# Probabilities transposed into the score banks, and each group's work in another order

## The reference

```
xn = ln(x, g_norm)
q = l2norm(heads(xn @ Wq)) * q_scale;  k, v = split(xn @ Wkv);  k = l2norm(k) * k_scale
sim = 8 * q @ k.T + bias;   causal mask;   attn = softmax(sim)       # 16 heads, 256 x 257
y = ln((attn @ v) @ Wout, g_out)
out = x + down(quant(silu(gate(quant(y))) * up(quant(y))))
```

## Time and profile before

| | |
|---|---|
| median of 3 runs | 312.78 us (311.99 to 313.17) |
| the profiled execution | 312.39 us; its span (first to last instruction) 310.6 us |
| busy share of the span | TensorE 83%, VectorE 78%, ScalarE 73%, GpSimd 67% |
| granted TensorE clock, mean | 0.98 |
| values of groups 2 to 33 | from 38.6 to 270.6 us |

### The profile page before, as it was taken

How to read it: one execution, slowest core, us unless ns; L and a number is a source line. 1 busy time by engine, 2 the same in 40 slices (tenths; PEclk the granted TensorE clock), 3 DMA queues, 4 the chain that set the end, 5 groups by cost and what they waited for, 6 DMA issues and landing times.

```text
span 310.6 us, 7321 instructions
## 1 busy us (share of the span) xinstructions
PE 258.5 (83%) x2175; PEld 203.0 (65%) x2176; DVE 242.8 (78%) x967; ACT 226.9 (73%) x779; POOL 207.2 (67%) x394
## 2 busy tenths in 40 slices
PE   0668899999989998999899989999999987776260
PEld 0337677777877786778777877788778766561050
DVE  2989688777888788878877987787877766759993
ACT  1265689778877887788888878888788868448480
POOL 2789867777777777777777777777777655212301
PEclk9999999999999999999999999999999999999956
DMA  4279000000000000000000000000000020000013
GB/s 142 51 179 251 1 0 3 2 0 3 1 2 0 4 1 2 0 3 1 2 2 1 4 0 2 0 4 0 2 1 3 1 72 1 2 0 0 1 36 106
DMA packets 13083, 6.89 MB, mean 22 GB/s; under 512 B 1953, under 2 KB 12913, under 8 KB 13042
## 3 DMA queue, kind: packets, MB, share of 16 engines
q1 hardware_dynamic: 12466, 6.13, 7.4%
q10 hardware_dynamic: 576, 0.26, 0.3%
HBM read 5.31 MB, written 1.07 MB: 21 GB/s over the span
## 4 chain that ended last, share of the span: by engine, by line
PE 33%; DVE 27%; POOL 14%; ACT 12%; issue 10%; DMA 2%; ACTq 0%; POOLq 0%; DVEq 0%
PE bank L698 6%; POOL rq L388 6%; PE trans L837 6%; ACT prob L548 6%; PE bank L820 5%; PE trans L890 5%; DVE qn L1048 5%; DVE score L1181 5%; PE bank L794 4%; POOL prob L435 3%; PE bank L682 2%; ACT sq L505 2%; DVE hmax L1306 2%; ACT pT L559 2%; DMA g0b<-in_L_cond_g_dram 2%
## 5 line engine op out<-in xcount | busy, mean ns | idle before, releaser
L435 POOL TENSOR_SCALAR prob<-prob,rrow 128x258 f32<-128x258 f32 x254 | 106.0, 436 | 47.8 <-DVE rrow L1189 44.8
L548 ACT ACTIVATE prob<-score,negmax 128x258 f32<-128x258 f32 (+1 forms) x256 | 114.1, 451 | 30.9 <-DVE negmax L1181 30.9
L1181 DVE CUSTOM_DVE_ANT_0 score<-bank,bias 128x258 f32<-128x258 f32 (+1 forms) x256 | 77.9, 353 | 0.8 <-PE bank L820 0.6
L559 ACT COPY pT<-trans 128x384 f32<-128x384 f32 x124 | 52.9, 475 | 11.5 <-PE trans L890 11.3
L890 PE MATMUL trans<-ident,prob 128*128 128x128 f32 x372 | 55.3, 274 | 1.7 <-ACT kv L484 1.0
L388 POOL TENSOR_TENSOR rq<-qn,neghalf 128x8 f32<-128x8 f32 x32 | 54.3, 1697 | 2.7
L837 PE MATMUL trans<-pT,val 128*64 128x256 f32 (+1 forms) x512 | 48.7, 332 | 3.9 <-ACT pT L559 2.3
L820 PE MATMUL bank<-kT,qT 64*128 64x258 f32 (+1 forms) x512 | 51.1, 338 | 0.2 <-DVE qT L1053 0.2
L548 ACT ACTIVATION_READ_ACCUMULATOR prob<-score,negmax 128x1 f32 x256 | 49.2, 192 | 0.0
L837 PEld LDWEIGHTS trans<-pT,val 128*64 128x64 f32 x512 | 31.7, 136 | 25.1 <-ACT pT L559 10.7
L820 PEld LDWEIGHTS bank<-kT,qT 64*128 64x128 f32 x512 | 41.8, 187 | 8.9 <-issue 5.9
(11 more groups left out here) (188 smaller groups left out, 355.4 us busy)
## 6 DMA issues: line engine op xcount, KB each, us to landing
bias<-relative_table SPq DMA_DIRECT2D x8, 256.0 KB, 4.8
out_dram<-prob SPq DMA_DIRECT2D x4, 256.0 KB, 3.0
X<-in_x_dram SPq DMA_DIRECT2D x1, 896.0 KB, 12.2
prob<-in_L_cond_Wq_dram SPq DMA_DIRECT2D x1, 512.0 KB, 5.8
wout<-in_L_cond_Wout_dram SPq DMA_DIRECT2D x1, 512.0 KB, 13.5
prob<-in_L_ffn_w_down_dram SPq DMA_DIRECT2D x1, 176.0 KB, 2.5
X<-in_x_dram SPq DMA_DIRECT2D x1, 128.0 KB, 4.6
prob<-in_L_ffn_w_gate_dram SPq DMA_DIRECT2D x1, 128.0 KB, 2.1
```

The costliest lines, as they stand in the source:

```text
L435: pool.tensor_scalar(prob[:, par, h, cols], prob[:, par, h, cols], rrow[:, par, h, t:t + 1], 1.0, ALU.mult, ALU.mult).then_inc(normed, 1)
L548: act.activation(prob[:, par, h, cols], score[:, h % 4, cols], ACT.Exp, scale=-1.0, bias=negmax[:, par, h, t:t + 1], accum_out=rowsum[:, p ...
L559: act.copy(pT[:, h % 4, :], ps[:, 0:3 * P]).then_inc(pT_ready, 1)
L1181: dve.tensor_tensor_reduce(score[:, h % 4, c0:c0 + w], ps[:, c0:c0 + w], bias[:, h, 0:w], -1.0, -3.0 * NEG, ALU.add, ALU.min, negmax[:, pa ...
```

## The change

- The probabilities of head i are transposed into score bank i, once VectorE has read the new scores of head i out of it. ScalarE's copy empties it, and the next scores follow it through the values' wait.
- That frees two banks: values are in 4, q's products in 5, q's transposes in a bank of their own, 6. q's products no longer wait for the copy of the transposes.
- TensorE: y's products go ahead of the turns, all four turns stand together, q's transposes behind them, q's products last. The waits for the small transposes' copies (`low_out`) stand before the next scores.
- VectorE: heads 0, 1, 2, q's normalisation, head 3, inversion, the copy of q's transposes. The small work stands at the group's end: k's norm in the group before, x's low half behind g3 and ahead of x's statistics, y's statistics at the end of g1, y's maximum in g2.
- ScalarE: the exponential of head 1 ahead of all four copies of transposed probabilities.
- Only for the last sequence, y's transposes and the null column go to q's transpose bank.

```diff
-        score_ps, trans_ps = bank[0:4], bank[4:6]
-        val_ps, q_ps, misc = bank[5], bank[6], bank[7]
-        tails = trans[:, :, 3 * P:4 * P]
+        front, back = psum("front", 2), psum("back", 2)
...
+        score_ps = bank[0:4]
+        val_ps, q_ps, qT_ps, misc = bank[4:8]
+        front_tails, back_tails = front[:, :, 3 * P:4 * P], back[:, :, 3 * P:4 * P]
...
@@ ScalarE, group(s)
+                if s.live:
+                    exponent(heads(s.at)[1])
                 if s.turned is not None:
                     pT_evac(s.turned, 0)
                     pT_evac(s.turned, 1)
...
-                if s.live:
-                    exponent(heads(s.at)[1])
                 if s.turned is not None:
                     pT_evac(s.turned, 2)
                     pT_evac(s.turned, 3)
@@ TensorE, turn(s, i)
+                if s.live:
+                    pe.wait_ge(scored, 2 * (heads(s.at)[i][0] + 1))
...
-                elif g > 1:
-                    pe.wait_ge(pT_ready, g - 1)
-                if i == 1 and s.summed is not None:
-                    pe.wait_ge(oT_ready, s.summed + 1)
                 if i < 2:
                     low_make(s, i)
-                if i == 2:
-                    low_out(s)
...
-                ps = bank[i] if last else trans_ps[i % 2]
                 for k, c0 in enumerate((KEYS1 + 1, P + 2, 1)):
-                    product = pe.transpose(ps[:, k * P:k * P + P], prob[:, par, h, c0:c0 + P], ident[:, :])
+                    product = pe.transpose(bank[i][:, k * P:k * P + P], prob[:, par, h, c0:c0 + P], ident[:, :])
@@ TensorE, group(s)
+                if s.at > 1:
+                    low_out(Group(s.at - 1))
...
+                if s.summed is not None:
+                    y_products(s.summed, 0)
+                    y_products(s.summed, 1)
+                if s.g == 1 and s.prev is not None:
+                    y_null(s.prev)
                 if s.turned is not None:
                     turn(s, 0)
                     turn(s, 1)
-                if s.summed is not None:
-                    y_products(s.summed, 0)
+                if s.turned is not None:
+                    turn(s, 2)
+                    turn(s, 3)
                 if s.quarter is not None:
                     qT_make(s.quarter)
...
                 if s.made is not None:
-                    pe.wait_ge(qT_ready, s.made)
@@ VectorE, group(s)
-                if s.g == 2 and s.prev is not None:
-                    y_stats(s.prev)
-                if s.kT is not None:
-                    k_norm2(s.kT)
                 if s.quarter is not None and s.quarter >= 4:
                     q_norm2(s.quarter, s.quarter % 4)
-                if s.g == 0 and s.prev is not None and s.next is not None or s.at == 1:
-                    xT_split_low(s.next, s.next % 2)
+                if s.kT is not None:
+                    k_normalise(s.kT)
                 if s.summed is not None:
                     oT_copy(s.summed)
...
-                    score_pair(heads(s.at)[0:2])
+                    score_pair(heads(s.at)[0:3])
                 if s.quarter is not None and s.quarter >= 4:
                     q_normalise(s.quarter, s.quarter % 4, q_ps)
                 if s.live:
-                    score_pair(heads(s.at)[2:3])
+                    score_pair(heads(s.at)[3:4])
+                    invert(heads(s.at)[0:2])
                 if s.quarter is not None:
                     qT_evac(s.quarter, s.quarter % 4, s.quarter // 4 % 2)
...
                 if s.at == 1:
+                    xT_split_low(1, 1)
                     null_values()
+                if s.kv is not None:
+                    k_norm2(s.kv)
...
+                if s.g == 1 and s.prev is not None and s.live:
+                    y_stats(s.prev)
+                if s.g == 2 and s.b > 1:
+                    yT_absmax(s.b - 2)
+                if s.g == 3 and s.prev is not None and s.b + 2 < B:
+                    xT_split_low(s.b + 2, s.b % 2)
                 if s.g == 3 and s.b + 3 < B:
                     x_stats(s.b + 3)
```

More of the change, by code:

```diff
@@ L234, in psum, with y_turned, null_out @@
             return ctx.enter_context(nc.psum_tensor(name, [P, banks, 512], F32))
[L236 to L239, removed]
-        score_ps, trans_ps = bank[0:4], bank[4:6]
-        val_ps, q_ps, misc = bank[5], bank[6], bank[7]
-        tails = trans[:, :, 3 * P:4 * P]
+        front, back = psum("front", 2), psum("back", 2)
+        bank = [two[:, i, :] for two in (front, back) for i in range(2)]
+        bank += [psum(f"bank{i}", 1)[:, 0, :] for i in range(4, 8)]
+        score_ps = bank[0:4]
+        val_ps, q_ps, qT_ps, misc = bank[4:8]
+        front_tails, back_tails = front[:, :, 3 * P:4 * P], back[:, :, 3 * P:4 * P]
         def halves(ps):
             return ps[:, 0:N].rearrange("p (t c) -> p t c", t=2)
+        def y_turned(m):
+            return front_tails if m < B - 1 else halves(qT_ps)
+        def null_out(m):
+            return back_tails[0:H, :, :] if m < B - 1 else halves(qT_ps[0:H, :])
         def y_out(t):
@@ L557, in pT_evac @@
                     act.wait_ge(o_done, at)
-                ps = bank[i] if at == GB * B - 1 else trans_ps[i % 2]
-                act.copy(pT[:, h % 4, :], ps[:, 0:3 * P]).then_inc(pT_ready, 1)
+                act.copy(pT[:, h % 4, :], bank[i][:, 0:3 * P]).then_inc(pT_ready, 1)
             def null_evac(m):
                 act.wait_ge(n_done, m + 1)
-                act.copy(halves(pnT[0:H, :]), tails[0:H, :, :]).then_inc(n_ready, 1)
+                act.copy(halves(pnT[0:H, :]), null_out(m)).then_inc(n_ready, 1)
             def wT_evac(k):
@@ L673, in yT_make @@
                     pe.wait_ge(y_norm, 2 * (m + 1))
-                product = pe.transpose(tails[:, t, :], yn[:, t, :], ident[:, :])
+                product = pe.transpose(y_turned(m)[:, t, :], yn[:, t, :], ident[:, :])
                 if t == 1:
@@ L697, in qT_make @@
                     head_pair = qn[:, 2 * k:2 * k + 2, :].rearrange("p a d -> p (a d)")
-                    last = pe.transpose(q_ps[:, k * P:k * P + P], head_pair, ident[:, :])
+                    last = pe.transpose(qT_ps[:, k * P:k * P + P], head_pair, ident[:, :])
                 last.then_inc(qT_done, 1)
@@ L777, in null_weights @@
                 at = KEYS1 if t == 0 else 0
-                product = pe.transpose(tails[0:H, t, :], prob[:, m % 2, :, at], ident[:, :])
+                product = pe.transpose(null_out(m)[:, t, :], prob[:, m % 2, :, at], ident[:, :])
                 if t == 1:
@@ L871, in turn @@
                     pe.wait_ge(normed, 2 * g + 2)
[L872 to L875, removed]
-                elif g > 1:
-                    pe.wait_ge(pT_ready, g - 1)
-                if i == 1 and s.summed is not None:
-                    pe.wait_ge(oT_ready, s.summed + 1)
                 if i < 2:
                     low_make(s, i)
-                if i == 2:
-                    low_out(s)
-                if i >= 2 and s.null is not None and not last:
+                if i >= 2 and s.null is not None and s.live:
                     if i == 2:
@@ L919, in group @@
                     keep_busy(6, bank[5])
[L920 to L926, removed]
                 if s.turned == GB * B - 1:
+                    pe.wait_ge(qT_ready, GB * B)
                     for t in range(2):
@@ L1263, in group @@
                 if s.at == 1:
+                    xT_split_low(1, 1)
                     null_values()
+                if s.kv is not None:
+                    k_norm2(s.kv)
                 if s.at == 2:
                     x_normalise(2)
-                if s.g == 0 and s.b > 1:
-                    yT_absmax(s.b - 2)
+                if s.at == GB:
+                    xT_split_low(2, 0)
                 if s.g == 0 and s.prev is not None and s.b + 2 < B:
                     x_normalise(s.b + 2)
+                if s.g == 1 and s.prev is not None and s.live:
[4 more added lines that the diff above has]
+                    xT_split_low(s.b + 2, s.b % 2)
                 if s.g == 3 and s.b + 3 < B:
@@ L1280, in group @@
                     ffn_weights(3)
+                    yT_absmax(B - 2)
                 if s.at == GB * B + 1:
```

22 lines of the change are left out of this document (8 added, 14 removed).

## The result

The changed kernel takes 319.49 us (median; 315.81 to 320.61), the kernel before 312.91 in the same comparison: slower, ratio 1.017 with a 95% interval of 1.013 to 1.022 (one disturbed execution of the changed kernel, 320.61, is left out of the ratio). The forecast was 318.6 us, slower. It is slower beyond the noise, but the interval leaves open whether by more or less than 2%. Its profiled execution took 318.85 us with a span of 317.1, against 310.6.

What follows compares the result with a forecast made beforehand. TensorE's work was taken as the floor, with q's round setting g0 to g2; the change closes a longer round. 3.8 + 0.7 - 0.3 + 1.6 = 5.8 us more gives 318.6 us, range 311.0 to 323.5.

Steps and rivals of the forecast that it cites:

- round, g3: Last of a batch's four groups: loop from q products through inversion, scores, turn 3, q's transposes; 7.31 us, was 6.83.
- g2: Third group of a batch: the 7.31 us round plus 0.62 for y's normalisation, 7.93 us where 7.62 was.
- g1: Second group of a batch: chain through k's squares, GpSimd's k power, inversion and scores, 7.56 us where 7.66 was.
- g0: First group of a batch: chain through x's statistics, GpSimd's powers and normalisation, null transposes; 8.52 us where 8.46 was.
- opening with groups 2 and 3: Kernel's start: x's low half behind the copy of q's transposes, 1.2 us once; groups 2 and 3 longer; together 1.6.
- The wait ahead of turn 3: TensorE in g2 and the group after it: idles for the score pass, 0.5 to 0.8 us each.
- argument from 151.08: Against the no-difference rival: TensorE's null transposes in g0 already waited for GpSimd's normalisation, until 151.08 us in the profile.
- x's normalisation: VectorE in g1, beside GpSimd's power: 0.57 long taken; with 0.90 instead, the total would be 1 us more.
- TensorE's work: Rival: TensorE's own work sets the pace, most of 1.71 us a batch goes, 304 us; chance 0.13.
- deciding point: Last group of a batch: TensorE reaches turn 3 at 5.1 us, fourth score released at 5.6; 0.5 earlier means no wait.
- The rival without difference: Rival: the GpSimd chain in g0 doesn't bind, a batch falls to 30.1 us, total 312.3; chance 0.12.
- ScalarE's copies of pT: Rival: these copies end 0.3 to 0.5 us late in g0 and g2, a batch gains 1, total 323.5; chance 0.07.

Runs made afterwards that it cites:

- experiment 2: The changed kernel with q's four transposes ahead of turns 2 and 3 instead of behind turn 3: 306.54 us, ratio 0.979 to the kernel before.
- Experiment 4: The changed kernel with q's normalisation back behind two heads' scores, heads 2 and 3 after it: 317.70 us, ratio 1.015 to the kernel before.
- experiment 3: The changed kernel with x's statistics ahead of VectorE's wait for q's transposes: 314.67 us, ratio 1.005 to the kernel before.

## Why the prediction was right, point by point

| term | forecast | measured |
|---|---|---|
| round, g3 | 7.31 | 7.24 |
| g2 | 7.93 | 7.78 |
| g1 | 7.56 | 7.40 |
| g0 | 8.52 | 8.62 |
| batches 1 to 5, more than before | 3.8 | 2.2 |
| batch 6 | 0.7 | 0.4 |
| batch 7 and the end | -0.3 | 0.2 |
| opening with groups 2 and 3 | 1.6 | 3.7 |
| sum | 5.8 | 6.5 |

**The round** is right in place and nearly in size, and experiment 2 shows it by taking one term out of it. Of its nine terms seven came within 0.01. Turn 3 took 0.39 until the next start where 0.33 was forecast, and q's transposes 0.35 where 0.49 was: the 0.49 was read behind a wait, and without one they take less. These two errors partly cancel. The wait ahead of turn 3 was forecast at 0.5 to 0.8 us and is 0.30 in g3 and 0.37 in g2: in g3 TensorE gets there 5.33 us into the group (173.22 to the end of turn 2 at 178.55), not 5.1. Experiment 4 shows that three heads, q's normalisation and one head sum alike in both orders. g2's term for y's normalisation was 0.08 too high, since the inversion's 0.17 until its successor is 0.10 when y's pass follows it.

**g0** is right: the chain over GpSimd (experiment 3). The low half took 0.47 until its successor, not 0.34, and null transposes and turns 0.87, not 0.79; two shorter terms make up for half of that, and 0.1 is left. The prediction's argument from 151.08 was weaker than it says, since TensorE was not idle there before.

**g1** was 0.16 too high. k's squares took 0.29, not the 0.51 that I read at 153.01. There the normalisation of GpSimd ran beside them; now GpSimd waits for them.

```profile
157.45 0.69 DVE L1050 COPY qT<-bank 128x512 f32<-128x512 f32 x1 [2.05 <-PE bank L704]
158.05 0.22 DVE L1022 CUSTOM_DVE_ANT_0 ksq<-kv 128x64 f32<-128x64 f32 x1
...
158.34 0.60 DVE L1011 TENSOR_SCALAR xn<-X,mv,rstd 128x128 f32<-128x128 f32 x2
```

This is VectorE of the changed kernel at the end of g0. x's normalisation took 0.60 for two, as I had chosen, not the 0.90 of the batches before. All sixteen instructions of that line take 0.336 to 0.345 us in the changed kernel. I had kept both cases for x's normalisation and not thought of k's squares, which read two operands from the on-chip memory. The Trainium skill (SBUF — State Buffer, Who interferes with whom) says that such a VectorE instruction contends with GpSimd's reads, and a pass in a two-port mode with all of GpSimd's accesses; both durations agree with it.

**The opening** is where the sum was off most, by 2.1 us; batches 1 to 6 were off by 1.9 the other way. Of the added waits 15.70 - 14.10 = 1.6 us lie ahead of group 2, where 1.2 was forecast, and 0.5 in groups 2 and 3, where 0.4 was. One of them was not foreseen: I had x's low half only (the wait ahead of q's products, 1.38 us in the changed kernel's first trace), and the larger wait, 1.85 us, is turn 0 of group 1 for VectorE's first pass of that group. In the kernel before, TensorE waited 0.30, 0.16 and 1.04 in this group. The rest, some 1.6 us, is the slow stretch ahead of the second q transposes (26.05 us against 24.48), which I hadn't counted; that it is TensorE's clock is inferred from the lengths of the products, not shown by the granted clock. The total came out within 1 us by luck, because these errors cancel; direction and groups did not need it.

**The rivals.** TensorE's work does not set the pace of the changed kernel, but its deciding point was real: where turn 3 comes later or the transposes don't stand behind it, the pace is nearly TensorE's and the time is 306.5, near that rival's 304. The rival without difference fails on g0, 8.62. ScalarE's copies of pT cost nothing more in the steady groups: there only the weight loads of the values wait for them, 0.36 to 0.43 us before and 0.36 to 0.37 after. In the last batch and right behind it TensorE waits 0.62 to 1.02 us for them before and 0.96 to 1.16 after.

## What to carry to other kernels

An instruction that is put behind another in an in-order queue inherits its wait. Draw the round that closes over all engines, add its terms from the trace, and compare it with the busiest engine's work before moving anything: here one set of transposes on the wrong side of one wait made the difference between 2% slower and 2% faster. When a buffer is shared with a new reader, the order around it must be chosen again, and the spare work belongs ahead of the wait that it doesn't need. Where an engine waits, look further down its queue for small work that is ready and that another engine needs: x's statistics, moved into such a wait, gave 1 us a batch.

## What the runs showed of the hardware

In the opening the same program runs at different TensorE speeds in different executions. The second and third pair of the first q products took 1.77 to 2.08 us in some executions and 1.02 to 1.13 in others, of kernels that are the same up to there. Each of the two pairs takes 1.9 times as long at its slowest as at its fastest (2.08 against 1.12, 1.92 against 1.02), near the ratio of the clock's two levels, 2.4 and 1.2 GHz, though the windows of the slow ones show a granted clock of 1.00 in some traces and of 0.50 in others. No run changes anything ahead of them, so what decides it stays open.

In three of the nine profiled executions with the new banks the granted clock fell to 0.50, the level of 1.2 GHz, somewhere between 34 and 43 us, behind a wait of 1.85 us in group 1. Where q's first products fell into that stretch the first of them took 0.76 and 0.77 instead of 0.47 us, and in those two executions 2.2 us more passed from the second q transposes to the values of group 2 (17.90 against 15.70). In two other executions with the same wait the clock did not fall. Nor did it in the four in which the wait was shorter (1.54 to 1.64) or mostly filled (0.39 left). What decides it among equal waits stays open.
